# An attention loop on TensorE: the products with the probabilities placed between a step's second and third score

## The reference

```
q, k, v = x Wq + bq, x Wk + bk, x Wv + bv        (32 heads of 16)
scores  = q k^T / sqrt(16), causal               (1024 x 1024 for each head)
out     = softmax(scores) v
return    out Wo + bo
```

## Time and profile before

| what | us |
|---|---|
| runs, median of 3 (lowest, highest) | 684.83 (684.49, 686.05) |
| the profiled execution | 683.69 |
| its span | 681.9 |
| TensorE busy, matmuls / weight loads | 613.8 (90%) / 404.4 (59%) |
| VectorE busy | 377.8 (55%) |
| ScalarE busy | 293.3 (43%) |
| GpSimd busy | 77.0 (11%) |
| mean granted clock of TensorE | 0.956 |

### The profile page before, as it was taken

How to read it: one execution, slowest core, us unless ns; L and a number is a source line. 1 busy time by engine, 2 the same in 40 slices (tenths; PEclk the granted TensorE clock), 3 DMA queues, 4 the chain that set the end, 5 groups by cost and what they waited for, 6 DMA issues and landing times.

```text
span 681.9 us, 9359 instructions
## 1 busy us (share of the span) xinstructions
PE 613.8 (90%) x3688; PEld 404.4 (59%) x3688; DVE 377.8 (55%) x555; ACT 293.3 (43%) x509; POOL 77.0 (11%) x106
## 2 busy tenths in 40 slices
PE   2999999999999997974798987999999999998993
PEld 2788888878888874763566665434444444444441
DVE  5676553266543354622367457478898798822025
ACT  3456342133422222211321114577777677775540
POOL 3000000000000018100000222121211212121100
PEclk9999999999999997998799997599999899999996
DMA  6313313101111020469751001441633610100003
GB/s 218 123 63 124 122 64 124 62 32 62 43 52 62 32 79 15 125 206 178 266 181 32 3 1 31 75 95 36 111 75 65 108 30 18 26 20 17 21 18 135
DMA packets 24304, 53.64 MB, mean 79 GB/s; under 512 B 8880, under 2 KB 9392, under 8 KB 24256
## 3 DMA queue, kind: packets, MB, share of 16 engines
q1 hardware_dynamic: 23844, 52.33, 28.2%
q0 software_dynamic: 288, 0.58, 0.4%
q10 hardware_dynamic: 128, 0.13, 0.1%
HBM read 39.77 MB, written 10.61 MB: 74 GB/s over the span
## 4 chain that ended last, share of the span: by engine, by line
PE 75%; DVE 9%; DMA 7%; ACT 6%; issue 2%; SPq 1%; ACTq 0%; DVEq 0%
PE bank L1155 11%; PE bank L1138 10%; PE slot L894 8%; PE bank L894 7%; PE slot L896 7%; PE slot L895 7%; PE bank L896 7%; PE bank L895 7%; DMA heads_dram<-attn_lo 6%; PE slot L1061 5%; ACT probs L872 4%; PE slot L1069 2%; DVE maxcol L1460 2%; DMA stage<-in_stream 1%; PE slot L910 1%
## 5 line engine op out<-in xcount | busy, mean ns | idle before, releaser
L872 ACT ACTIVATE probs<-bank 128x512 f32<-128x512 f32 (+2 forms) x320 | 155.6, 560 | 71.4 <-PE bank L1138 69.6
L1460 DVE TENSOR_REDUCE maxcol<-slot 128x2 f32<-128x1024 f32 (+2 forms) x112 | 125.0, 1142 | 44.8 <-PE slot L1069 23.4
L894 PE MATMUL slot<-xt_hi,ring_hi 128*128 128x512 f32 (+2 forms) x248 | 99.7, 402 | 22.1 <-DVE attn_lo L1416 18.6
L895 PE MATMUL slot<-xt_lo,ring_hi 128*128 128x512 f32 (+2 forms) x248 | 98.4, 397 | 0.0
L896 PE MATMUL slot<-xt_hi,ring_lo 128*128 128x512 f32 (+2 forms) x248 | 98.2, 396 | 0.0
L1138 PE MATMUL bank<-qst,kst 50*128 50x512 f32 (+3 forms) x288 | 79.9, 444 | 6.8 <-ACT probs L872 5.9
L1155 PE MATMUL bank<-probs,v_sb 128*32 128x512 f32 (+3 forms) x768 | 85.4, 519 | 0.1
L1138 PEld LDWEIGHTS bank<-qst,kst 50*128 50x128 f32 x288 | 36.8, 199 | 68.2 <-ACT probs L872 59.4
L894 PEld LDWEIGHTS slot<-xt_hi,ring_hi 128*128 128x128 f32 (+2 forms) x248 | 47.4, 191 | 35.2 <-issue 22.0
L1061 PE MATMUL slot<-kst,qst 48*128 48x512 f32 (+3 forms) x288 | 58.3, 397 | 7.7 <-DVE maxcol L1460 7.6
L690 POOL TENSOR_SCALAR_AFFINE_SELECT probs<-probs 128x512 f32<-128x512 f32 x64 | 41.8, 653 | 200.9 <-ACT probs L872 200.9
(11 more groups left out here) (186 smaller groups left out, 880.8 us busy)
## 6 DMA issues: line engine op xcount, KB each, us to landing
stage<-in_stream SPq DMA_DIRECT2D x43, 512.0 KB, 3.5
heads_dram<-attn_hi SPq DMA_DIRECT2D x8, 512.0 KB
heads_dram<-attn_lo SPq DMA_DIRECT2D x8, 512.0 KB
qst<-heads_dram SPq DMA_DIRECT2D x12, 256.0 KB, 5.7
kst<-heads_dram SPq DMA_DIRECT2D x12, 256.0 KB, 9.7
stage<-u_sb SPq DMA_DIRECT2D x64, 32.0 KB, 2.0
out_y<-x_sb SPq DMA_DIRECT2D x8, 256.0 KB, 2.2
stage<-den_dram SPq DMA_DIRECT2D x15, 128.0 KB
```

What stands on the lines that cost most here:

```text
L872: act.activation(probs[:, to:to + heads, 0:n], bank[b % 3][:, 0:heads * n].rearrange("p (h n) -> p h n", n=n), ACT.Exp, scale=HD ** -0.5). ...
L894: pe.matmul(out_ap, a[0], b[0], start=start, stop=False)
L895: pe.matmul(out_ap, a[0], b[1], start=False, stop=False)
L1460: dve.tensor_reduce(per_head[:, :, slots[0]:slots[-1] + 1], scores, AX.X, ALU.max).then_inc(S["max_free"], 1)
```

## The change

The condition that places the products in a step's loop over its four places. `hh` is the place, `GH - 1` is 3.

```diff
                         k = STEPS * g + s - LAG
-                        if hh == GH - 1 and k >= 0:
+                        if hh == 1 and k >= 0:
                             weigh_values(k)
             for k in range(STEPS * GROUPS - LAG, STEPS * GROUPS):
                 weigh_values(k)
```

## The result

The changed kernel takes 725.91 us in the median of four executions (713.41 to 743.54), the kernel before beside it 685.44. The comparison of the two gives a ratio of 1.0466 (95% interval 1.0351 to 1.0582), on 684.83 us some 717. The ratio counts only the two quicker executions, 713.41 and 722.00 us; in the other two TensorE spent more time at its lower clock. I had forecast 704.5, with a range up to 721. The direction is right and the ratio lies inside the range; the median of the four executions lies above it. What is new is the spread, 30 us where the four executions of the kernel before spread over 3. (With more of both the contrast is smaller and stays: 14 executions of the changed kernel spread over 49 us, 51 of the kernel before over 12.) The profiled execution took 713.41 us with a span of 711.7.

A forecast was written before the change was run, and what follows sets the result against it. No engine is full; scores wait for exponentials because three banks serve four scores. +23 (groups 1 to 5) +2 (group 0) -2.0 -3.4 (groups 6, 7) = +19.6 on 683.69, so 703.3, median 704.5 us; range 695 to 721.

The forecast's parts named there:

- The ring of three banks: Three banks serve four scores, so the next step's second score waits for the third exponential; groups 1 to 5: +23 us.
- C: Time from a step's third score to the next step's second score, between 0.45 and 1.25 us.
- VectorE's reductions fit the longer group: VectorE's 23.93 us of reductions per group were taken to fit into the longer group.
- narrow steps: Four of a group's twelve steps, at most 256 columns, no wait today; the change adds about 0.8 us each.
- The copy: A half's first values' product waits for ScalarE's accumulator copy, 2.0 us after the third score; twice a group.
- Group 0: First group, mostly at 1.2 GHz, where small gaps cover more of the wait: +2 us, between 0 and 4.
- Groups 6 and 7: Last groups, whose output matmuls fill the wait after the change: -2.0 us for group 6, -3.4 for group 7.
- the transition with output products: Groups 6 and 7: longer of C + lone score and pair + output matmuls + 0.23, plus 0.10 and products.
- The clock: TensorE: the sum assumes waits do not lower the clock; the rival that it falls: +20 us, 724, chance 0.15.
- signs of being wrong: Groups 1 to 5 at 28 us, narrow steps without following waits, or attention at granted clock 0.5 beyond group 0.
- only the large gap would change place: Rival: narrow steps and copies stay free, groups 6 and 7 gain 6 to 8 us: 680, chance 0.05.
- no new wait would come: Rival: the fourth score's wait goes and none comes, -25 us: 660, chance 0.02.

## Why the prediction was right, and where it was not

**The ring of three banks**, right. C was put at 1.25, 1.08, 1.14 and 0.86 for 512, 384, 256 and 128 columns and measures 1.18, 1.02, 1.13 and 0.86; a group of 1 to 5 was put at 32.6 us and is 32.4 to 32.8 at the full clock. Five of them are 163.3 us against my 163; over the 139.9 of the kernel before that is +23, and +24.6 over 138.7, what its groups take without their own short stretch at the lower level. Two errors cancel a little inside the group: most steps came out up to 0.1 short, and steps 5 and 11 are 0.5 and 0.4 longer than their sums, by VectorE's slots, though I had written that VectorE's reductions fit the longer group. That narrow steps are the largest part is shown by the run that spares them (3.6 us of 4.6 in group 5, some 0.5 of it the copy's wait in step 2).

**The copy**, right as a mechanism and near in size: the product at 1.98 against 2.0 after the third score; removing its wait gives 0.5 us a group.

**Group 0**, right: 34.98 us by its exponentials against 33.00, +2.0.

**Groups 6 and 7**, right in sign, too large: -5.4 was forecast, -3.2 measured when they alone are changed. In the changed kernel group 7 is 34.0 us instead of 32.65, so -2.0. Group 6 is 36.80 there, with 6.8 us at the lower level; even at 0.5 us for each of these it would be 33.4, so that the forecast's 32.4 is missed by 1 us or more, and most of its -2.0 is not there. The term that was mis-sized is the transition with output products. TensorE in order of time, group 6, steps 8 and 9:

```profile
645.25 0.50 PE L1138 MATMUL bank<-qst,kst 50*128 50x512 f32 x2
645.68 1.07 PE L1155 MATMUL bank<-probs,v_sb 128*32 128x512 f32 x8
646.68 0.49 PE L1138 MATMUL bank<-qst,kst 50*128 50x512 f32 x2
647.10 0.50 PE L894 MATMUL slot<-xt_hi,attn_hi 128*128 128x512 f32 x1
...
648.69 0.33 PE L1138 MATMUL bank<-qst,kst 50*128 50x128 f32 x2
```

A pair of scores takes 0.43 before products (I had 0.23 + 0.10) and 0.42 before output matmuls (I had 0.34), so each such transition is 0.2 longer, some fourteen times. In step 11 of both groups and steps 4 and 5 of group 7 the fourth score waits besides (in group 6 the output matmuls start 0.88 behind the third score of step 11, not 0.42), since the products before are the short ones. For group 7 I had forecast no wait at the fourth scores.

**The clock**, the step that failed. I wrote that "by the rows, in which such waits did not lower the clock in groups 3 or 7, the sum stands", and kept the fall of the clock as a rival at 0.15. It fell too, not in place of the forecast's waits but on top of them, and stretches of attention at a granted clock of 0.5 beyond group 0 were one of my own signs of being wrong. T is 119 us in the mean of 14 executions against 67 for the kernel before, and at 0.30 the 52 us more are 16 of the 42.5 us between the mean spans, 727.1 and 684.6. My price for a us at the lower level, 0.36, measures 0.30 to 0.32 over whole executions and 0.45 in a short stretch. The rows of group 3 and 7 could not carry the step: they showed the clock up beside some 4 us of waits in 28, and I asked them about 9 in 33. The Trainium skill, "TensorE: Matmul & The Clock Gate", section "A second HAM failure mode: psum-queue depth-cycling", describes this for a bf16 kernel: short idle stretches while TensorE cycles through PSUM banks make the clock fall and rise. The traces agree in part: in one profile of the changed kernel the clock falls once in each of groups 2 to 5, in another not once in 160 us, and with the gap filled it holds behind the first low stretch in both profiles.

**The sum.** At an equal clock the change costs 26.8 us (709.4 - 682.6), or 25.4 with the changed kernel's own slope of 0.32. Added up by group at the full clock behind group 0, as an estimate from the profiles, it is some 24: +2.0, +24.6, 0 to -1 for group 6, -2.0 for group 7. Against the forecast of 19.6 that is 2 to 3 us more in groups 6 and 7 and 1.6 in groups 1 to 5; the 1 to 3 us that remain lie within the error of the clock's correction. The number itself came out inside the range with some luck: the ratio leaves out the two executions that lost most to the clock, and the mean of all 14 lies above 721, by the clock. I had also written that a measurement can tell 0.2% from nothing; the kernel before alone spreads over 12 us. The rivals by which only the large gap would change place, or no new wait would come, fall with the narrow steps' waits.

**Open.** Why in one execution the clock falls in groups 4 and 5 and in another it holds through the same work is not settled: the engines' busy times there are the same. Nor is it settled why the low stretch that begins with group 0 lasts 24 us in two profiles of the changed kernel and 72 in the third. It was not tried whether a fourth score bank would free the order altogether.

## What to carry to other kernels

Count the waits that an order makes possible before moving work: here a ring of three banks means that whatever stands between the write of a bank and its next write must last 1.2 us (0.9 for 128 columns), and the order before had eight such places a group, the new one twelve. Put short independent work into the gap that waits anyway, as the output products behind the second score (1.2% faster), and keep the long work where it covers the most. When the executions of a kernel begin to scatter, compare at an equal granted clock before explaining microseconds.

## What the runs showed of the hardware

I had not expected waits of 0.3 to 0.6 us, repeated every 2 to 3 us, to cost clock: T rises from 67 to 119 us in the mean, up to 209, and 24 more matmuls a group in the waits bring it back to 84. They make a fall likelier and do not force it: one execution held 2.4 GHz for 160 us beside the same waits. One us at the lower level costs this kernel 0.30 us over whole executions (0.45 in a stretch of 3.4 us), not 0.5, probably because much of a step's loop is ScalarE's time and the way between the engines, which the level does not change; that reason was not tested by itself.
